# A two-layer decoder on one core: PSUM results of the attention preparation are evicted in the step that makes them

## The reference, cut to what matters

```
Qh = heads(x @ Wq + bq)            # 100 x 256 per sequence
Kh = heads(ctx @ Wk + bk)          # 361 x 256 per sequence
Vh = heads(ctx @ Wv + bv)
attn = softmax(Qh Kh^T / sqrt(16)) # layer 1: keys with mask == 0 left out
x = layernorm(x + (attn Vh) @ Wo + bo)
```

## Time and profile before

| | us |
|---|---|
| median of 3 runs | 1727.98 (1725.83 to 1728.22) |
| profiled execution | 1723.14 |
| its span, first to last instruction | 1721.4 |
| PE busy | 1220.6 (71%) |
| DVE busy | 1164.5 (68%) |
| POOL busy | 940.7 (55%) |
| ACT busy | 802.7 (47%) |
| chain that ended last: PE, DVE, ACT, issue, POOL | 39%, 29%, 12%, 11%, 8% |
| mean granted TensorE clock | 0.856 of 2.4 GHz |

### The profile page before, as it was taken

How to read it: one execution, slowest core, us unless ns; L and a number is a source line. 1 busy time by engine, 2 the same in 40 slices (tenths; PEclk the granted TensorE clock), 3 DMA queues, 4 the chain that set the end, 5 groups by cost and what they waited for, 6 DMA issues and landing times.

```text
span 1721.4 us, 17263 instructions
## 1 busy us (share of the span) xinstructions
PE 1220.6 (71%) x5876; PEld 696.2 (40%) x5876; DVE 1164.5 (68%) x1627; ACT 802.7 (47%) x1738; POOL 940.7 (55%) x802
## 2 busy tenths in 40 slices
PE   5677777765448678775876767867766778787753
PEld 2444444432124344442433434434343445454432
DVE  1556666663187987978879789798896345554456
ACT  0254444442545556455574555745643144545540
POOL 3600000010187997979979789798799134333405
PEclk8689999996668889898898998989997878989875
DMA  5000010000400501205013040130300300000000
GB/s 169 18 10 10 9 55 1 1 1 1 164 26 1 186 0 60 106 2 185 1 40 126 1 162 26 39 127 0 135 19 1 86 25 13 13 13 1 2 0 20
DMA packets 21029, 79.89 MB, mean 46 GB/s; under 512 B 4273, under 2 KB 7417, under 8 KB 19961
## 3 DMA queue, kind: packets, MB, share of 16 engines
q1 hardware_dynamic: 20942, 78.79, 13.2%
HBM read 77.55 MB, written 1.23 MB: 46 GB/s over the span
## 4 chain that ended last, share of the span: by engine, by line
PE 39%; DVE 29%; ACT 12%; issue 11%; POOL 8%; DMA 1%; SPq 0%; DVEq 0%; ACTq 0%; POOLq 0%
PE ps L484 37%; DVE ps L1515 5%; DVE arena L1519 4%; DVE hstat L866 3%; POOL arena L1435 3%; DVE arena L1486 3%; ACT arena L690 2%; DVE arena L1517 2%; PE ps L548 2%; POOL arena L1446 2%; ACT ps L1336 2%; DVE arena L1502 1%; ACT arena L700 1%; DVE arena L853 1%; ACT arena L1296 1%
## 5 line engine op out<-in xcount | busy, mean ns | idle before, releaser
L484 PE MATMUL ps<-arena 128*32 128x100 f32 (+11 forms) x3184 | 540.8, 408 | 252.3 <-issue 60.4
L484 PE MATMUL ps<-arena,ident 128*128 128x400 f32 x1024 | 398.7, 542 | 121.7 <-DVE arena L1517 66.7
L1435 POOL TENSOR_TENSOR arena<-arena 128x1600 f32<-128x1600 f32 x128 | 466.5, 3661 | 0.0
L484 PEld LDWEIGHTS ps<-arena 128*32 128x32 f32 (+9 forms) x3184 | 267.4, 157 | 476.2 <-issue 215.4
L1336 ACT ACTIVATE ps<-arena 128x400 f32<-128x400 f32 x512 | 281.5, 588 | 284.7 <-DVE arena L1517 246.7
L484 PEld LDWEIGHTS ps<-arena,ident 128*128 128x128 f32 x1024 | 207.6, 207 | 305.2 <-DVE arena L1517 81.3
L1515 DVE TENSOR_TENSOR_SCAN ps<-ps,arena 128x800 f32<-128x800 f32 x144 | 262.5, 1823 | 41.1 <-POOL arena L1435 26.3
L1446 POOL TENSOR_TENSOR arena<-arena 128x1600 f32<-128x1600 f32 x56 | 200.0, 3571 | 107.9 <-DVE arena L1519 107.2
L690 ACT ACTIVATE arena<-ps,hstat 100x361 f32<-100x361 f32 x256 | 144.8, 567 | 196.8 <-DVE hstat L866 196.8
L1519 DVE TENSOR_TENSOR_SCAN arena<-ps,arena 128x800 f32<-128x800 f32 x112 | 197.6, 1806 | 29.7 <-ACT ps L1336 24.6
L460 POOL TENSOR_SCALAR stat<-stat 100x1 f32<-100x1 f32 x48 | 9.8, 204 | 365.4 <-DVE stat L445 365.2
(11 more groups left out here) (170 smaller groups left out, 1218.8 us busy)
## 6 DMA issues: line engine op xcount, KB each, us to landing
arena<-bc_scratch SPq DMA_DIRECT2D x64, 800.0 KB, 5.5
arena<-in_ctxT SPq DMA_DIRECT2D x16, 361.0 KB, 3.1
arena<-in_w_in SPq DMA_DIRECT2D x4, 1024.0 KB, 8.2
arena<-in_expT SPq DMA_DIRECT2D x1, 2048.0 KB
arena<-in_w_out SPq DMA_DIRECT2D x4, 512.0 KB, 3.2
arena<-in_mask SPq DMA_DIRECT2D x8, 141.0 KB
wo<-in_L_Wo SPq DMA_DIRECT2D x2, 512.0 KB
arena<-in_xT SPq DMA_DIRECT2D x1, 800.0 KB
```

The source lines that it names most:

```text
L484: return nc.tensor.matmul(outp, lhsT, rhs, start=first, stop=last)
L1435: nc.gpsimd.tensor_tensor(bx[:, unit % BX].rearrange("p (j t) -> p j t", j=SEGMENT), bbc[:, nq].rearrange("p (j t) -> p j t", j=SEGMENT), ...
```

## The change

Six entries of `AT` change. The keys are evicted at the step of PE's product instead of one later, so are the values, the queries of both layers, and the turned rows XT and FT of layer 1. PE's list, the banks, all operands and all semaphores stay as they are; only the place of the evictions in ACT's and DVE's streams changes.

```diff
 AT = {
     "K": (0, 1),
     "V": (2, 3, 4),
-    "Kc": (1, 2),
-    "Vc": (3, 4, 5),
+    "Kc": (0, 1),
+    "Vc": (2, 3, 4),
     "Q": 6,
-    "Qc": 7,
+    "Qc": 6,
...
     "1XT": 7,
-    "1XTc": 8,
+    "1XTc": 7,
     "1Q": 9,
-    "1Qc": 10,
+    "1Qc": 9,
...
     "1FT": 11,
-    "1FTc": 12,
+    "1FTc": 11,
```

## The result

The changed kernel takes 1704.6 us (median of four runs, 1704.0 to 1709.6), beside 1726.9 for the kernel before on the same chip: a ratio of 0.9878, interval 0.9858 to 0.9898. The same kernel run again beside the experiments took 1701.7 beside 1727.7, 0.9852 (0.9833 to 0.9872). So it is 22 to 26 us faster; the forecast was 19. One run of the values alone took 1794 us at a lower granted clock (0.748) and is left out of every ratio; the profile used for that kernel is of its second series. The page of the first profile of the change says

A forecast was written before the change was run, and what follows sets the result against it. PE was held to wait for unread results because products share three banks, on the path setting a sequence's time. Gains of 16.8 us (layer 0) and 2.3 (layer 1), 19.1 together, gave 1708.9 us, range 1699 to 1720.

The forecast's parts named there:

- Keys: Layer 0, sequences 2 to 6: earlier key evictions end PE's waits before K1 and V0; step 4's scores 2.39 us earlier.
- rival (c): Key evictions at ACT's head delay exps until exp 3 holds up step 4's scores; 4.1 us slower, 1732; chance 0.05.
- Values: DVE, both layers: V0's eviction still waits; V1's, ahead of step 4's maxima, costs 0.34 us in each of 13 sequences.
- the idleness ahead of SM: Layer 0, PE's wait before SM: grows by 0.34 us through V1's eviction, with the low clock behind it taken as unchanged.
- Queries: Layer 0, steps 6 to 8: evictions fill DVE's idle 2.34 us, T follows O, step 8's maxima come 0.97 us earlier.
- Layer 1: Layer 1, sequences 0 to 6: all moved evictions together gain 2.3 us, from -2 to 4.5.
- +1.2, -2.0 and +0.6: Layer 1, six sequences: 0.2 us gained by early keys, 0.34 lost to V1's eviction, 0.1 gained at O's wait, each.
- The sum: Whole kernel: 16.8 us gained in layer 0, of it 15.1 in sequences 2 to 6, and 2.3 in layer 1: 19.1.
- The clock: Layer 0, behind PE's idleness before SM: the 1.2 GHz stretch stays unchanged; 8 us either way over five sequences.
- Rival (a): Layer 0: some of the gain is given back to the clock, leaving 11 us, 1717; chance 0.14.
- a slow O in each sequence: Layer 0: O at 3.5 us in each sequence would show that the clock took back some of the gain.
- Rival (b): Low-clock stretch vanishes or moves onto idleness, and K1, V0 give their weight loads too: 28 us, 1700; chance 0.10.

## Why the prediction was right

**Keys.** K1 and V0 start without an idle, as said, and exp 3 is not what releases step 4's scores, so rival (c) fell. Size: 2.62 a sequence instead of 2.39. Starting from K0, K1 comes 1.35 us earlier (1.34 said) and V0 another 1.20: its wait of 1.05 and the 0.15 for the weight load that was left out.

**Values.** V0's wait held (1.66 us behind the scores), and the price of V1 ahead of the maxima was 0.32 instead of 0.34. The step was right, and its question was too small. The prediction saw that nothing passes a waiting eviction (and 7.46 us of DVE's idleness in the earlier trace rows), and took that as given because the change didn't alter it. The kernels with values behind the maxima show that this same wait was worth more than everything the change touches. In layer 1 nearly all of the gain stands in the quads in which quantising moves into the idleness that the earlier trace rows show. A smaller slip: the idleness ahead of SM was to grow by 0.34, and grew by 0.17 (2.08 to 2.25), since the context rows on ACT (L719), and not V1's eviction, now end it.

**Queries.** T follows O directly, and the second to the third maxima take 9.57 (9.6 predicted). The 9.57 rest on luck in part. The walk had SM slow and O fast (1.67 and 1.89 us, as before); in the profile that gave 9.57, SM is fast and O slow (0.94 and 3.10), and the quad's mean granted clock is about the same (0.82, and 0.84 before). With no low stretch in the quad it takes 9.13 with the late queries (keys alone, sequences 3 and 5) and 7.93 with the early ones (first profile, sequences 4 to 6), so there the order is worth 1.20.

**Layer 1.** It gained 5.2 us, not 2.3, so it ends outside the forecast's bound of 4.5. Its rows gave 0.23 each, exactly. With keys and values moved as well the layer is no faster than with its own rows and queries alone (251.5 and 251.7); +1.2, -2.0 and +0.6 had been summed for them, about 0, and the difference agrees with that; the single terms were not measured. The excess is sequence 0's third quad, 8.66 us before and 5.94 after, and it goes with the granted clock (0.50 and 0.95). The prediction put the change of layer 1's clock at nothing without a reason, and this layer's time differs by 3.5 us where its order is the same (before and the queries alone).

**The sum.** Sequences 2 to 6 gave 16.8 instead of 15.1, sequences 0 and 1 2.1 instead of 1.7, and first maxima that come 2.1 later took as much back. The mechanism was right, the place of the low clock apart, and the forecast was 4 us off the median of the first runs (1704.6) and 7 off the second (1701.7).

**The clock.** Here the working was lucky. It took the low stretch as unchanged and bounded it by 8 us either way. For the whole change that holds: 18.8 or 26.9 us of it instead of 16.4. For the parts it doesn't: with the queries alone the stretch grew by 26 us and cost 12.9, well over the bound, and turned the gain of 5.4 into a loss. And the two profiles of one kernel differ by 8 us at 1.2 GHz and 4.8 us in layer 0's time, so the place of the stretch varies from one execution to the next. Rival (a) had a slow O in each sequence as its sign. O was at 1.89 us in the first profile, where the logits and experts behind XT slowed instead; in the second it is there (3.10 us in all five sequences, at a granted clock of 0.58), and yet those sequences take 37.5 us, 3.4 less than before, since SM and the experts' group were fast. So the sign didn't tell the rival from the forecast. Rival (b)'s vanished stretch came where the gaps were filled, and nearly so (3.8 us) with only the values behind the maxima. The section of the Trainium skill cited at (a) ties the high clock to dense matmuls; the gaps that it warns of are longer than the ones removed here, so that their removal would raise the clock was the prediction's own step. The kernel with two gaps filled fits it (0.0 us). The keys alone and the queries alone don't: they take idleness away and get more of the low clock (36 and 42 us instead of 16). Nearer to what these runs show is another section of the same page of the Trainium skill, TensorE: Matmul & The Clock Gate, A second HAM failure mode: psum-queue depth-cycling: cycling through banks leaves short idle times between groups of matmuls, often enough that the clock goes down and up again. Such short idle times are in all these traces; whether the three shared banks are what matters was not tried.

What stays open: why a given order, and one execution of it rather than another, puts the low stretch on SM, on O, on the experts or on several of them. The runs show that filling both idle times removes it. They don't show that an idle time of this size brings it by itself: in the keys alone 2.08 us ahead of SM stand in all five sequences, and in two of them the clock stays at 1.00.

## What to carry to other kernels

An instruction in an in-order queue that waits for work of a later step holds everything behind it: look for the longest idle time in front of such an eviction, ask what useful work stands behind it, and move the eviction behind that, later than its operand allows (here one entry, 38 us). Moving evictions earlier pays only where the wait for their bank is on the path, and only where nothing urgent stands behind them. And don't judge the parts of a reordering by timing each alone where matmul runs at two clocks, and don't trust one profile of each: four parts whose ratios multiply to 1.001 gave 0.985 together.

## What the runs showed of the hardware

Stretches at 1.2 GHz came in a loop in which the longest idle times of PE were 1.6 to 2.9 us: 4 to 44 us of some 200, in nine kernels with the same instructions in another order. Where the cost could be set apart it was 0.35 to 0.49 us for each us, by a count that is good to 2 us. Filling one idle time left as much of it (18.8 us), filling both removed it (0.0), and 71 more matmul records took 8.2 us less. Two executions of one kernel had 26.9 and 18.8 us of it, on different instructions. Two evictions of 128x256 one behind the other hold DVE for 0.67 us until the next instruction starts, one alone for 0.34.
